# Per-head exponentials with a bias instead of a matmul that subtracts the peak; second norm inside the attention loop, last tokens under the shared network

## The chip, the cores and the metric

One core of one Trainium2 chip runs the whole kernel in one launch. The metric is the time of one execution in microseconds (us) on the device, the median of several runs. Engines are named as the profile names them: PE is TensorE (PEld its weight loads), DVE is VectorE, ACT is ScalarE, POOL is GpSimd, SP issues most of the DMAs.

## The reference

The input `x` has 16 blocks of 128 tokens, each token with 256 features.

```
x = x + tanh(g_xattn) * xattn(layernorm(x), ctx)     # 16 heads of 16 features in each block of 128 tokens
    attn  = gamma * (Q K^T / 4) + delta * (alpha_pos * max(D,0) + alpha_neg * min(D,0))
    D     = clip(frac_k - frac_q, -0.2, 0.2);   probs = softmax(attn);   out = probs V;   out @ Wo.T + bo
x = x + tanh(g_ffn) * ffn(layernorm(x))
    8 experts (256 -> 1024 -> 256, exact gelu), the best 2 of each token by the gate's scores,
    weighted with the softmax over these 2, and a shared network of the same size for every token
```

Every matrix product is made of three bf16 products (high by high, high by low, low by high part), so each operand is split: ACT makes the high part with a copy, DVE or POOL subtracts it to get the low part.

## The kernel before, in words

The program is written out by hand for each engine, with semaphores; each engine works through its own list in order. A wait at the head of a list holds everything behind it. It has these stages.

1. Projections of keys, values and queries.
2. Attention: a loop over 32 half blocks `u`, two for each block `b` of 128 tokens (a token block below). Each `u` has two groups of four heads, so `n = 2u` and `2u+1`, each a tile of 128 queries by 4x128 keys. PE makes scores (`scores`), DVE takes the largest of each head (`peaks`, L830), turns it to two bf16 parts (L833, L835), PE turns these round (`turn_peaks`), ACT copies them (`peaks_moved`, L631), PE subtracts them from the scores with two 512-column matmuls (`subtract_peaks`), ACT takes one exponential of 128x512 (`exponent`, L623), PE turns the result round (`turn_probs`, L1270), ACT copies the high part (`probs_high`, L627), DVE the low part (`probs_low`, L840), PE multiplies with the values (`weigh_values`). Once for each block there follow `output`, `turn_o`, `outputs_high`, `outputs_low`, `project_o`, `residual`. ACT and POOL also convert one piece of the expert weights for each block (`piece_high`, L619; `piece_low`, L487), and prepare the differences of the bias table (`clip`, L472 and L473; `top_part`, L653; `split_difference`, L480).
3. The second norm, its transposition and the gate's scores in eight pairs of blocks (`norm2`, `turn2`, `high2`, `low2`, `gate`), after the attention loop.
4. The shared network: 32 steps `m` (4 groups of 512 tokens by 8 parts of the hidden width). PE runs `shared_up(m+2)` and `shared_down(m)`, six 512-column and twelve 256-column matmuls. ACT makes the gelu (L725) and its high part (L734), POOL (the first 8 steps) or DVE the low part. Beside it DVE chooses the experts, counts the rows of each, and gives every row a place (L990 to L1047); PE's step 8 needs DVE's split, which in DVE's list stands behind this choice. Then DVE builds the rows (`payload`) and POOL sends them out with indirect DMAs (L544). Further weight pieces are loaded (SP, L347: piece `m` waits until piece `m-2` is converted, as there are two buffers) and converted.
5. The experts: 39 tiles of 128 rows (`body`). PE runs up(j), turns tile j+2, and down(j-1).

A weight piece is 128x1024 of fp32, 512 KB; there are 36 of them, four for each network. `store_group` writes the result of the shared network, and `b2f` (1 MB, L425) is loaded by SP when the last of these four writes has landed.

## Time and profile before

| | |
|---|---|
| median of 3 runs | 586.01 us (585.37 to 590.19) |
| the profiled execution, its own time | 587.57 us |
| its span in the trace | 585.7 us |
| mean granted clock of PE | 0.953 of full speed |

The span is what the trace shows of that execution; the 1.9 us beside it lie before and after. Differences are worked out within the span and then applied to the median.

### The profile page before, as it was taken

To read this page: it belongs to the slowest core of one execution; us is meant where nothing else is said; L and a number is where in the kernel's file an instruction comes from. 1 tells how busy PE (TensorE), PEld (TensorE's weight loads), DVE (VectorE), ACT (ScalarE), POOL (GpSimd) and SP (SyncE) were. 2 spreads that over 40 slices of the span, in tenths; PEclk is the share of its full clock that TensorE was granted. 3 is DMA by queue.
4 is the path that set the end of the run, shared out by engine and by line. 5 is a ranking of instruction groups with operands and counts; after the bars stand their busy time and mean duration, and the time that the engine had idled before them with its cause. 6 is when DMAs were issued, how large, how long until landed. Compare 5 with 4: busy or idle time off the path is not lost.

```text
span 585.7 us, 17314 instructions
## 1 busy us (share of the span) xinstructions
PE 516.2 (88%) x6424; PEld 421.7 (72%) x6425; DVE 408.1 (70%) x972; ACT 309.3 (53%) x722; POOL 262.1 (45%) x193
## 2 busy tenths in 40 slices
PE   2698699899999997599679999999999999999990
PEld 0354477777777776456346668899999999999990
DVE  4965648787878788969848748666666666666660
ACT  3656546666666665468336665444544544444430
POOL 4344527575757653459566624322323323323322
PEclk9889969999999999879798999999999999999996
DMA  9500012233323341134253685322223233222121
GB/s 278 199 1 5 1 41 88 65 106 120 96 69 102 118 130 37 41 105 139 87 172 126 197 179 186 66 45 54 38 51 54 36 53 54 36 54 53 28 29 18
DMA packets 37554, 49.17 MB, mean 84 GB/s; under 512 B 8066, under 2 KB 30722, under 8 KB 37380
## 3 DMA queue, kind: packets, MB, share of 16 engines
q1 hardware_dynamic: 30356, 39.18, 22.5%
q0 software_dynamic: 7152, 9.34, 8.7%
q8 instruction: 33, 0.54, 0.4%
q14 instruction: 13, 0.11, 0.1%
HBM read 31.79 MB, written 16.72 MB: 83 GB/s over the span
## 4 chain that ended last, share of the span: by engine, by line
PE 64%; DVE 23%; ACT 4%; DMA 3%; issue 3%; POOL 1%; SPq 0%; POOLq 0%; DVEq 0%; ACTq 0%
PE bank L1172 59%; DVE mx L830 4%; DVE W L840 3%; PE bank L1270 3%; DVE W L805 2%; PE bank L1433 1%; ACT W L627 1%; DVE m L833 1%; DMA xres<-x 1%; DVE xres L861 1%; DVE hbuf L960 1%; DVE st L863 1%; DVE xres L812 1%; DMA xres<-xs_dram 1%; POOL rstd L444 1%
## 5 line engine op out<-in xcount | busy, mean ns | idle before, releaser
L762 ACT ACTIVATE hbuf<-bank,b1t 128x128 f32<-128x128 f32 x312 | 88.7, 368 | 112.2 <-PE bank L1172 109.6
L1172 PE MATMUL bank<-W,xT 128*128 (+1 forms) x1704 | 136.5, 249 | 0.4 <-DVE xT L1128 0.4
L1172 PE MATMUL bank<-xres,W 128*128 128x128 bf16 (+1 forms) x1920 | 124.7, 224 | 9.5 <-DVE xres L812 9.2
L563 POOL DMA_INDIRECT out<-xres,idu x39 | 60.7, 1557 | 156.3 <-DVE xres L1147 147.2
L1172 PEld LDWEIGHTS bank<-xres,W 128*128 (+1 forms) x1920 | 111.9, 98 | 18.6 <-issue 8.8
L1172 PEld LDWEIGHTS bank<-W,xT 128*128 128x128 bf16 (+1 forms) x1704 | 113.9, 97 | 14.4 <-issue 1.0
L1172 PE MATMUL bank<-W 128*128 128x17 bf16 (+3 forms) x1440 | 86.2, 207 | 3.2 <-DVE W L840 1.5
L1172 PEld LDWEIGHTS bank<-W 128*128 128x128 bf16 x1440 | 67.8, 98 | 16.6 <-DVE W L840 2.7
L487 POOL TENSOR_TENSOR W<-stage,W 128x1024 bf16<-128x1024 f32 x28 | 60.6, 2167 | 39.8 <-ACT W L619 31.8
L1172 PE MATMUL bank<-W,hsplit 128*128 128x256 bf16 x432 | 57.3, 283 | 9.3 <-DVE hsplit L1089 5.5
L1172 PEld LDWEIGHTS bank<-W,hsplit 128*128 128x128 bf16 x432 | 43.7, 102 | 24.1 <-DVE hsplit L1089 6.2
L840 DVE TENSOR_TENSOR W<-bank,W 128x512 bf16<-128x512 f32 x64 | 41.3, 686 | 26.2 <-ACT W L627 26.2
L1128 DVE TENSOR_TENSOR xT<-hbuf,xT 128x512 bf16<-128x512 f32 x78 | 54.0, 693 | 2.7
L1172 PE MATMUL bank<-xT,W 128*128 128x512 bf16 x192 | 51.3, 409 | 0.0
L1126 DVE CAST xT<-hbuf 128x512 bf16<-128x512 f32 x78 | 34.4, 441 | 21.1 <-ACT hbuf L762 19.5
L830 DVE TENSOR_REDUCE mx<-bank 128x4 f32<-128x512 f32 x64 | 40.9, 680 | 7.7 <-PE bank L1172 7.7
L544 POOL DMA_INDIRECT xs_dram<-W,place x32 | 36.8, 1150 | 19.1 <-DVE W L1059 10.2
L623 ACT ACTIVATE W<-bank 128x512 f32<-128x512 f32 x64 | 34.7, 594 | 19.2 <-PE bank L1172 19.2
L1270 PE MATMUL bank<-cst,W 128*128 128x128 f32 x256 | 41.1, 285 | 0.3 <-ACT W L623 0.3
L725 ACT ACTIVATE hbuf<-bank,col 128x512 f32<-128x512 f32 x32 | 21.9, 683 | 35.9 <-PE bank L1172 17.0
L619 ACT ACTIVATE W<-stage 128x1024 bf16<-128x1024 f32 x36 | 37.5, 1043 | 3.4 <-DMA stage<-wts 3.4
L480 POOL TENSOR_TENSOR W<-W 128x512 bf16<-128x512 f32 x16 | 18.5, 1156 | 43.2 <-ACT W L653 43.1
(153 smaller groups left out, 662.7 us busy)
## 6 DMA issues: line engine op xcount, KB each, us to landing
stage<-wts SPq DMA_DIRECT2D x36, 512.0 KB
xres<-xs_dram SPq DMA_DIRECT2D x39, 128.0 KB, 2.1
xs_dram<-hbuf SPq DMA_DIRECT2D x7, 645.0 KB, 6.5
W<-ctxT SPq DMA_DIRECT2D x4, 512.0 KB, 6.0
xres<-x SPq DMA_DIRECT2D x4, 512.0 KB, 7.9
out<-xres SPq DMA_DIRECT2D x4, 512.0 KB, 5.3
W<-wproj SPq DMA_DIRECT2D x4, 256.0 KB, 6.8
hsplit<-frac SPq DMA_DIRECT2D x16, 64.0 KB, 5.8
```

Of the source, the lines that this page charges most:

```text
L487: nc.gpsimd.tensor_tensor(lo, stage[:, k * HID:(k + 1) * HID], hi, ALU.subtract).then_inc(converted, 1)
L544: nc.gpsimd.indirect_dma_start(xs_dram, bass.IndirectOffsetOnAxis(place[:, b % 4, k:k + 1], axis=0), pay[:, b % 4, k, :], None).then_inc(d ...
L563: nc.gpsimd.indirect_dma_start(out, bass.IndirectOffsetOnAxis(idu[:, par, t:t + 1], axis=0), ysb[par][t], None, compute_op=ALU.add).then_i ...
L619: nc.scalar.activation(W[:, piece_at(i, k):piece_at(i, k) + HID], stage[:, k * HID:(k + 1) * HID], ACT.Copy).then_inc(conv_hi, 1)
L623: nc.scalar.activation(sc[n % R], psS[n % R][:], ACT.Exp).then_inc(probs, 1)
L762: ins = nc.scalar.activation(hbuf[:, q, c * TR:(c + 1) * TR], bank[UPS * par + q][:, c * TR:(c + 1) * TR], ACT.Gelu, bias=b1t[:, par, UC * ...
L830: nc.vector.tensor_reduce(mx[:, u % 2, HR * i:HR * (i + 1)], psS[n % R][:].rearrange("p (j t) -> p j t", t=T), AX.X, ALU.max).then_inc(pea ...
L840: nc.vector.tensor_tensor(pTl[n % 2], psT[n % 2][:], pTh[n % 2], ALU.subtract).then_inc(pt_lo, 1)
L1126: nc.vector.tensor_copy(hi, hbuf[:, q, :]).then_inc(h_hi, 1)
L1128: nc.vector.tensor_tensor(lo, hbuf[:, q, :], hi, ALU.subtract).then_inc(h_ready, 1)
L1172: return nc.tensor.matmul(o, a, b, start=start, stop=stop, **kw)
L1270: ins = nc.tensor.transpose(psT[n % 2][:, j * T:(j + 1) * T], sc[n % R][:, j * T:(j + 1) * T], ident)
```

## The change

- The weights of the queries are scaled with -gamma/4 and the slopes with -1, so that PE makes negated scores. DVE takes the smallest of each head. ACT takes the exponential of one head each (128x128) with scale -1 and this minimum as its bias, four instructions in the place of one. `turn_peaks`, `peaks_moved`, `subtract_peaks` and their tables go.
- The second norm runs inside the attention loop, one block at a time, two to three blocks behind: statistics on DVE (`stats2`, `aggregate2`), four small POOL instructions (`deviation2`), the norm itself on ACT (`norm2`, was DVE), `turn2`, `inputs2_high` and `inputs2_low`.
- After the loop PE starts the shared network at once. The gate's scores of the first 12 blocks, and the last block's output, norm and scores stand between its first steps (`last_tokens`).
- DVE chooses in two parts. The counting is made by PE (31 matmuls of 8 to 120 columns beside the one that was there, after step 5), and DVE's chain for it is shorter. DVE splits the hidden tiles from step 5 on (POOL did to step 7), and these splits stand between the parts of the choice.
- The conversions of weights move: pieces 16 to 19 stand at steps 3, 4, 6 and 8 on ACT and are finished on POOL (18 and 19 between the sending of rows); 20 to 31 stand at steps 10 to 28 on ACT, finished on DVE; 32 to 35 are converted inside the first four tiles of the experts on ACT and POOL, and are loaded after `b2f`.
- The loop over tiles is cut in two, so that PE waits for the last piece only at tile 16.

```diff
-POOL_PIECES_AT = (1, 3, 4, 6, 7)
-VECTOR_PIECES = range(PIECES - 12, PIECES - 4)
-HIGHS_AT = (10, 11, 13, 15, 18, 20, 22, 23)
-LOWS_AT = (11, 12, 14, 16, 19, 21, 23, 24)
-LAST_HIGHS_AT = (28, 30)
+POOL_PIECES_AT = (2, 3)
+DISPATCH_PIECES_AT = (1, 3)
+PIECES_AT = (3, 4, 6, 8)
+VECTOR_PIECES = range(NOW + 4, PIECES - 4)
+HIGHS_AT = (10, 11, 13, 14, 16, 17, 19, 20, 22, 24, 26, 28)
+LOWS_AT = (11, 12, 14, 15, 17, 18, 20, 21, 23, 25, 27, 29)
-POOL_SPLITS = HC
+POOL_SPLITS = 5
+RANKS_AT = 5
...
(sync)
             store_group(3)
             sp.wait_ge(out_written[3], 16)
             sp.dma_start(b2f, b2.to_broadcast([P, E * D])).then_inc(ld_b2, 16)
-            with sp.Fori(2, TILES // 2) as i:
+            load_pieces(PIECES - 4, PIECES - 2)
+            load_tile(4, 0)
+            load_piece(PIECES // 2 - 1, 0)
+            load_tile(5, 1)
+            load_piece(PIECES // 2 - 1, 1)
+            with sp.Fori(3, TILES // 2) as i:
...
(gpsimd)
+            def deviation2(b):
+                pool.wait_ge(ln2_stat, b + 1)
+                link(inverse_deviation(rstd2, mv2, b, b + 1))
+                link(nc.gpsimd.tensor_tensor(nmr2[:, b:b + 1], mv2[:, b:b + 1, 0], rstd2[:, b:b + 1], ALU.mult))
+                nc.gpsimd.tensor_scalar(nmr2[:, b:b + 1], nmr2[:, b:b + 1], -1.0, None, ALU.mult).then_inc(ln2_rstd, 1)
...
             for m in range(POOL_SPLITS):
+                if m == 2:
+                    deviation2(B - 1)
...
+                if b in DISPATCH_PIECES_AT:
+                    q = NOW + 2 + DISPATCH_PIECES_AT.index(b)
+                    piece_low(q // 2, q % 2)
...
-            add_tile(0, 0)
-            add_tile(1, 1)
+            for j in range(4):
+                piece_low((PIECES - 4 + j) // 2, j % 2)
+                add_tile(j, j % 2)
...
(scalar)
             def exponent(n):
-                act.wait_ge(sub_ps, n + 1)
-                nc.scalar.activation(sc[n % R], psS[n % R][:], ACT.Exp).then_inc(probs, 1)
+                act.wait_ge(peak, n + 1)
+                for j in range(HR):
+                    at = HR * (n % 2) + j
+                    ins = nc.scalar.activation(sc[n % R][:, j * T:(j + 1) * T], psS[n % R][:, j * T:(j + 1) * T], ACT.Exp,
+                                               scale=-1.0, bias=mx[:, n // 2 % 2, at:at + 1])
+                ins.then_inc(probs, 1)
...
+            def norm2(b):
+                act.wait_ge(ln2_rstd, b + 1)
+                if b:
+                    act.wait_ge(x2T_ps, b)
+                nc.scalar.activation(xh2, xres[:, b * D:(b + 1) * D], ACT.Identity,
+                                     scale=rstd2[:, b:b + 1], bias=nmr2[:, b:b + 1]).then_inc(xh2_ready, 1)
...
+                if m in PIECES_AT:
+                    q = NOW + PIECES_AT.index(m)
                     piece_high(q // 2, q % 2)
...
                 gelu_tile(j, par)
                 if more == 2:
                     high_tile(j + 2, par)
+                if isinstance(j, int) and j < 4:
+                    piece_high((PIECES - 4 + j) // 2, j % 2)
...
(vector)
+            choose(0, EARLY_TOKENS)
+            inputs2_low(B - 1)
+            link(choose(EARLY_TOKENS, B))
+            split_shared(5)
...
(tensor)
             piece_converted(pe, 3)
             shared_up(0)
             shared_up(1)
+            turn_o(B - 1)
+            turn2(B - 3)
+            gate(0, EARLY_TOKENS)
             for m in range(HC * GROUPS):
                 if m + 2 < HC * GROUPS:
                     shared_up(m + 2)
...
                 shared_down(m)
+                last_tokens(m)
```

## Rows read from the trace of the kernel before

**Rows 1.** Windows by stage: span, busy time and count of each engine, granted clock, DMA.

```profile
78.27:229.70 151.43, 141.06 (x2414) 116.50 (x2414) 119.53 (x258) 99.01 (x200) 88.60 (x55) 0.98 0.31 94
229.70:252.92 23.22, 13.60 (x211) 11.88 (x209) 21.03 (x54) 9.68 (x17) 10.52 (x8) 0.81 0.21 69
252.92:353.32 100.40, 91.11 (x577) 58.04 (x574) 72.67 (x199) 59.52 (x84) 62.47 (x48) 0.91 0.48 141
367.86:555.76 187.90, 187.90 (x2518) 177.75 (x2518) 123.11 (x309) 86.07 (x304) 53.61 (x35) 1.00 0.27 47
```

**Rows 2.** Timeline of PE in one token block of the attention loop.

```profile
158.79 0.66 PE L1270 MATMUL bank<-cst,W 128*128 128x128 f32 x4
...
161.05 1.20 PE L1172 MATMUL bank<-W 128*128 128x512 bf16 x26
...
163.57 0.22 PE L1172 MATMUL bank<-idb,m 128*16 128x128 bf16 x1 [0.61 <-DVE m L835]
```

**Rows 3.** Timeline of ACT in the same token block.

```profile
154.28 1.05 ACT L627 ACTIVATE W<-bank 128x512 bf16<-128x512 f32 x2
155.24 0.71 ACT L653 ACTIVATE W<-W,cst 128x512 bf16<-128x512 f32 x1
...
161.48 1.09 ACT L623 ACTIVATE W<-bank 128x512 f32<-128x512 f32 x2 [0.41 <-PE bank L1172]
```

**Rows 4.** Groups by line and form, ACT: busy us, mean ns of one, idle before.

```profile
L762 ACT ACTIVATE hbuf<-bank,b1t 128x128 f32<-128x128 f32 x312 | 88.7, 368 | 112.2 <-PE bank L1172 109.6 <-DVE xT L1128 2.3
...
L619 ACT ACTIVATE W<-stage 128x1024 bf16<-128x1024 f32 x36 | 37.5, 1043 | 3.4 <-DMA stage<-wts 3.4
...
L645 ACT ACTIVATE W<-xres,nmr,rstd 128x256 f32<-128x256 f32 x16 | 8.3, 589 | 16.9 <-POOL nmr L463 16.9
...
L637 ACT ACTIVATE W<-bank 128x256 bf16<-128x256 f32 x16 | 5.8, 360 | 1.2 <-PE bank L1292 1.2
```

**Rows 5.** Groups by line and form, POOL's powers.

```profile
L444 POOL TENSOR_TENSOR rstd<-rstd,mhalf 128x4 f32<-128x4 f32 x5 | 5.7, 1149 | 0.4
...
L444 POOL TENSOR_TENSOR rstd<-rstd,mhalf 128x12 f32<-128x12 f32 x1 | 2.3, 2297 | 0.1
```

**Rows 6.** Timelines of DVE and PE at the start of attention.

```profile
71.36 1.29 DVE L830 TENSOR_REDUCE mx<-bank 128x4 f32<-128x512 f32 x2 [2.00 <-PE bank L1172]
...
73.56 0.27 PE L1172 MATMUL bank<-idb,m 128*16 128x128 bf16 x1 [2.30 <-DVE m L835]
...
78.27 1.11 PE L1270 MATMUL bank<-cst,W 128*128 128x128 f32 x4 [0.26 <-ACT W L623]
...
99.41 0.60 PE L1270 MATMUL bank<-cst,W 128*128 128x128 f32 x4
```

**Rows 7.** Group by line and form: PE's down matmuls of the shared network.

```profile
L1172 PE MATMUL bank<-W,hsplit 128*128 128x256 bf16 x432 | 57.3, 283 | 9.3 <-DVE hsplit L1089 5.5 <-issue 3.5 <-POOL hsplit L533 0.3
```

**Rows 8.** Timeline of PE in the shared network, its up matmuls.

```profile
307.67 2.77 PE L1172 MATMUL bank<-xT,W 128*128 128x512 bf16 x6
...
328.13 1.46 PE L1172 MATMUL bank<-xT,W 128*128 128x512 bf16 x6
...
330.73 1.46 PE L1172 MATMUL bank<-xT,W 128*128 128x512 bf16 x6
```

**Rows 9.** Timelines of POOL and ACT: a conversion, a send, a load's wait.

```profile
269.42 2.13 POOL L487 TENSOR_TENSOR W<-stage,W 128x1024 bf16<-128x1024 f32 x1
...
284.03 1.35 POOL L544 DMA_INDIRECT xs_dram<-W,place  x1 [4.96 <-DVE W L1059]
...
274.76 1.06 ACT L619 ACTIVATE W<-stage 128x1024 bf16<-128x1024 f32 x1 [0.92 <-DMA stage<-wts]
```

**Rows 10.** Timelines of SP and PE at the experts' start; the issue of `b2f`.

```profile
362.20 0.33 SPq L425 DMA_DIRECT2D xres<-b  x1
...
363.99 2.85 PE L1172 MATMUL bank<-xres,W 128*128 128x128 bf16 x48
...
xres<-b SPq DMA_DIRECT2D x1, 1024.0 KB, 4.8
```

More of the change, by code:

```diff
@@ L59 @@
 C_I32 = C_TILE + TILES
-C_IND = C_I32 + KB
-C_POS, C_NEG, C_TOP, C_LOW, C_FLOOR, C_CEIL, C_SECOND = (C_IND + 2 * HR + k for k in range(7))
+C_POS, C_NEG, C_TOP, C_LOW, C_FLOOR, C_CEIL, C_SECOND = (C_I32 + KB + k for k in range(7))
 C_N = C_SECOND + 1
@@ L124, in build @@
         cab = [under(H * KB, bf16) for _ in range(2)]
-        ind = under(2 * HR * T, bf16)
-        mts = [under(T, bf16) for _ in range(2)]
         brows = under(4 * D, bf16)
@@ L282, in wait_alone, with tiles @@
             eng.sem_inc(passed[name], 1)
-        def tiles(eng, body):
-            body(0, 0, 2)
-            body(1, 1, 2)
-            with eng.Fori(1, TILES // 2 - 1) as i:
+        def tiles(eng, body, late=None):
+            for j in range(4):
+                body(j, j % 2, 2)
+            with eng.Fori(2, LATE_TILES // 2) as i:
+                body(2 * i, 0, 2)
+                body(2 * i + 1, 1, 2)
+            if late:
+                late()
+            with eng.Fori(LATE_TILES // 2, TILES // 2 - 1) as i:
                 body(2 * i, 0, 2)
@@ L565, in add_tile @@
                         ysb[par][t], None, compute_op=ALU.add).then_inc(added[t], 16)
-            add_tile(0, 0)
-            add_tile(1, 1)
-            with pool.Fori(1, TILES // 2) as i:
+            for j in range(4):
+                piece_low((PIECES - 4 + j) // 2, j % 2)
+                add_tile(j, j % 2)
+            with pool.Fori(2, TILES // 2) as i:
                 add_tile(2 * i, 0)
@@ L985, in _ @@
-            low2(PAIRS - 2, (PAIRS - 2) % 3)
-            low2(PAIRS - 1, (PAIRS - 1) % 3)
-            dve.wait_ge(gate_ps, B)
-            link(nc.vector.tensor_tensor(lg, bank[5][:, 0:B * E].rearrange("p (b e) -> p b e", e=E),
-                                         row[:, V_GB:V_GB + E].rearrange("p (o e) -> p o e", o=1).to_broadcast([P, B, E]), ALU.add))
-            for b in range(B):
-                ins = nc.vector.max(mx8[:, b, :], lg[:, b, :])
-            link(ins)
-            for b in range(B):
-                ins = nc.vector.max_index(ix8[:, b, :], mx8[:, b, :], lg[:, b, :])
@@ L997, in _, with split_shared @@
-            link(ins)
+            output(B - 1)
+            residual(B - 2)
+            stats2(B - 2)
+            aggregate2(B - 2)
+            outputs_low(B - 1)
+            inputs2_low(B - 3)
+            residual(B - 1)
+            stats2(B - 1)
+            aggregate2(B - 1)
+            inputs2_low(B - 2)
+            def split_shared(m):
+                dve.wait_ge(sh_hi, m + 1)
+                nc.vector.tensor_tensor(hsplit[:, m % DEEP, 1, :], hbuf[:, m % DEEP, :], hsplit[:, m % DEEP, 0, :],
+                                        ALU.subtract).then_inc(sh_ready[1], 1)
@@ new lines, in choose @@
+            def choose(lo, hi):
+                dve.wait_ge(gate_ps, hi)
+                link(nc.vector.tensor_tensor(lg[:, lo:hi], gate_bank(lo)[:, lo * E:hi * E].rearrange("p (b e) -> p b e", e=E),
+                                             row[:, V_GB:V_GB + E].rearrange("p (o e) -> p o e", o=1).to_broadcast([P, hi - lo, E]),
+                                             ALU.add))
+                for b in range(lo, hi):
+                    ins = nc.vector.max(mx8[:, b, :], lg[:, b, :])
+                link(ins)
+                for b in range(lo, hi):
+                    ins = nc.vector.max_index(ix8[:, b, :], mx8[:, b, :], lg[:, b, :])
+                return ins
@@ L1232, in scores @@
                     pe.wait_ge(d_ready, b + 1)
-                for i in (1, 0):
-                    if i == 0 and u:
-                        pe.wait_ge(mT_ready, u)
+                for i in range(2):
                     if u >= 2:
@@ L1303, in project_o, with turn2 @@
                 mm(psM[:, D:2 * D], oneb[:], brows[:, 3 * D:4 * D], False, True).then_inc(y_ps, 1)
+            def turn2(b):
+                pe.wait_ge(xh2_ready, b + 1)
+                if b >= B - 3:
+                    pe.wait_ge(x2_lo, b)
+                y = x2_ps(b)
+                for c in range(DC):
+                    ins = nc.tensor.transpose(y[:, c, :], xh2[:, c * P:(c + 1) * P], ident)
+                ins.then_inc(x2T_ps, 1)
             pe.wait_ge(ld_cst, 16)
```

355 lines of the change are left out of this document (152 added, 203 removed).

## The prediction

> **What bounds the kernel now.** I read the windows by stage first, then the timelines of each engine inside one stage, then the groups by line for durations. The windows [rows 1] show what matters where. In attention PE is busy 141.06 of 151.43 us. In the stage between (second norm and gate, 23.22 us) it is busy 13.60 us while DVE has 21.03: this is a bubble of PE. In the shared network it is busy 91.11 of 100.40, at a clock of 0.91. In the experts it is busy all the time, in a steady cadence with a clock of 1.00; the change doesn't touch what a tile costs there, so this stage moves as a whole.
>
> The attention loop takes (99.41 - 78.27) = 21.14 us for its first two token blocks [rows 6] and from there to the last pair's transposes at 229.70 [rows 1] it is 13.5 blocks, 9.65 to 9.72 each. In its timeline PE's instructions stand close together; the only gap is one of 0.61 for each block where it waits for the peaks on DVE [rows 2]. ACT has gaps before the exponentials [rows 3]. So PE and the chain of the peaks set the period of 9.72.
>
> **Part 1, exponentials by head.** PE loses, for each token block, four 512-column matmuls and two turned peaks. Of the 26 matmuls that start at 161.05, 24 are the small ones, so I take 0.21 for each of the two big ones: 4 x 0.21 = 0.85; two turned peaks with 0.15 each, and the 0.61 of waiting [rows 2]. It gains the two transposes of the second norm, 0.26. 9.72 - 0.85 - 0.3 - 0.61 + 0.26 = 8.2 us is what PE would need.
>
> ACT takes the bound over. Its nearest row to a 128x128 exponential with a bias is the experts' gelu: 368 ns for one, and 88.7/312 = 284 ns of busy time, so fours of 1.14 [rows 4]. A step from one to the next is (1.137 - 0.368)/3 = 0.256, so an exponent takes 4 x 0.256 = 1.03 of ACT, where the 512-wide one takes half of 1.09 less its overlap, 0.49 [rows 3]. For one block: four exponents 4.10; four copies of probabilities 4 x 0.48 = 1.92 (two in 1.05 with their tail) [rows 3]; the weight piece 0.94, the top part 0.61, the output 0.27, the new norm 0.50 and the new transposed copy 0.28, each its mean less 0.1 of overlap [rows 3, 4]. Sum 8.62. Of waits two remain: the second copy of a pair needs PE's transposes of the second exponent, 0.66 long [rows 2], while the first copy covers only 0.48 and the semaphores take 0.1 to 0.2, so some 0.37 twice. That is 9.36 for one block, ACT in one go. DVE loses the small peak instructions and gains two small ones; POOL gains `deviation2`, by interpolation from 1.15 for 4 columns and 2.30 for 12 [rows 5] 0.72 for the power and by estimate another 1.0 for the three small ones and their links: 1.7. POOL is busy for 88.60 of 151.43 us [rows 1], 5.7 for a block; with 1.7 it is 7.4. Both stay under 9.36. Behind POOL's wait for the statistics stands the split of the differences; it moves by 1 us and still comes 1 us before PE needs it, so I cost that at nothing.
>
> The page "ScalarE: Activation LUTs" of the Trainium skill (section on what ACT_TABLE_LOAD costs) says that an activation with a pointer for its bias takes about 280 ns + 0.833 ns for each element, with 93 ns of overlap: an estimate of 0.294 for a step. By this, which speaks against the change, the period would be about 10.0 and the loop slower than now. The rows have 0.256 for the same shape and operands, so the trace is better than the page here, and its number decides.
>
> So 13.5 blocks give 0.36 each, -4.9. The start of the loop gives more. Now the first peaks wait 2.30, the clock falls for ten us after it, and the first transposes start at 78.27 [rows 6]. After the change: first reduce 71.36 to 72.05, four exponentials 1.14, transposes at 73.25, -5.0. PE has the second scores in between and no long wait, so that I expect no fall of the clock there, and the first two blocks take 17.3 for 21.1 (ACT's cadence with less in it), -3.8. Together -13.7, by which the last pair's transposes start at 216.
>
> **Part 2, the stage between.** It goes. From the last pair's transposes to the first shared matmul there remain: the second exponent and its transposes 1.5, copy 0.57, low part 0.69, weighing 0.31, output projection 0.75, links: 4.5 for 23.2 [rows 1], -18.7. What is late next is the shared network's own feeding.
>
> **Part 3, shared network.** A step of PE is 2.60 (328.13 to 330.73) [rows 8]; from first up to last down 82. Now it takes 100.4 [rows 1]: 5.5 of waiting for DVE's choice and 3.5 of "issue" [rows 7], and some 8 at half clock behind these gaps and at its start (2.77 for 1.46) [rows 8]. The waiting for the choice goes (a split stands between its parts). Added to PE: twelve gates, four late ones, three norms' and one output's transposes, the projection and the counting, 16 x 0.27 + 1.0 + 0.75 + 1.2 = 7.3. The last block's chain (projection, residual, POOL, norm, transposes, gate) runs beside steps 0 to 3, each link ready when PE comes to it; I cost its waits at 0.5. If that cover failed, each us would count.
>
> New waits come from the weight pieces. ACT's list has piece 20 at step 10. Its load waits for piece 18 to be converted, and POOL does this only after sending the rows of block 1. I lay out the choice: scores of the last gate some 19 us after the shared network starts; max, index, one-hots to 24; counting on PE, then seven small DVE instructions, places, weights, first payload at 33.5. Four sends of 1.3 to 1.65 each, conversion 2.13, load 3.2 (from the end of a conversion at 271.55 to 274.76) [rows 9]: the piece lands at 45, while ACT is there at 34.5. ACT stands 10 us, and behind it the gelu of step 11; PE has two steps in hand and loses 3.1 at step 10 (DVE's table and accumulation before its split) and 4.5 at step 11. Piece 21 waits likewise for piece 19 behind blocks 2 and 3: 4.7 at step 12. After it, twelve pieces in two buffers with a turn-around of 3.2 + 1 + 1.2 are just above PE's cadence: 1.7 more. Sum 14.0, and 2.5 for the clock behind it. 82 + 7.3 + 0.5 + 14.0 + 2.5 = 106.3 against 100.4, +5.9. For the load I know 2.8 to 4.2, which makes 1.6 less or 3 more.
>
> **Part 4, start of the experts.** Before, the last pieces were through when tile 0 began. Now ACT has piece 32 behind the gelu of tile 0, and SP issues its load after `b2f`, which waits for the last write: 362.2 at its earliest, 4.8 to land, and the piece queued behind it some 1.7 more, so 368.7, less 1 since the write comes a little earlier. Conversion 0.94, half the gelu 1.14, its split 1.2: PE can go on with down(1) at 371, where it was at 363.99 [rows 10]. Some 0.6 of that is there already, as PE waited for tile 4. +6.5, and +2 for the clock behind a wait of 7 us. Pieces 33 to 35 come in time by the same layout. The bound from below is nothing (if the load were early), from above 11. The cut loop costs nothing, since PE is busy for the whole of the stage, over the exit of the loop that is there [rows 1].
>
> Sum: -13.7 - 18.7 + 5.9 + 8.5 = -18.0. Span 585.7 to 567.7, this execution, with the 1.9 beside its span, 587.57 to 569.6, the median of the runs, 1.6 lower, 586.01 to 568.0.
>
> **The rivals.**
> A. The loads are not late: the choice is quick enough, or the DMA queues empty enough, that parts 3 and 4 lose no more than half of 14 + 2.5 + 8.5. For it speaks that I stack many small durations; against it that piece 32 can't be loaded before the last write. 586 - 30 = 556, down to 550.
> B. PE's "issue" gap comes back. In the trace PE stood for 3.5 [rows 7] and ran at half clock behind it, 2.77 for 1.46 and a like loss after [rows 8], in the middle of the sending of rows. I left it out, since in the new order the sends are held up by payloads; with it, or with one more fall of the clock, 568 + 8 = 576, up to 582.
> C. The exponentials don't overlap as the gelus do, and ACT's step is the full 0.368. Then each block takes 16 x 0.112 = 1.8 more, 16 blocks 28.7: 597, slower. Its place is ACT in attention; it decides from 0.07 more for each instruction on, a step of 0.33. Against it stands the row of 312 gelus with the same source, target and bias [rows 4].
> D. PE's clock falls in the loop, as it is now busy 8.2 of 9.36. Rows of gaps of 0.61 have a clock of 0.98 to 1.00 [rows 1, 2], the falls followed gaps of 2.3 and more [rows 6 to 8]. A part of the loop at half clock costs 10 or more: about no change.
>
> **How the numbers follow.** Forecast 0.47 (561 to 574), A 0.2, B 0.2, C 0.05, D 0.05, the rest unnamed. A change of 1% (5.9 us) is about what a measurement of this kernel can tell from none. Faster by that: forecast, A, nearly all of B, 0.86; within it 0.08; slower 0.06. The range leaves out C, D and the far end of A: 551 to 582.
>
> **What would show it.** Right: a period of 9.4 in attention with ACT in one go and the gaps on PE waiting for ACT; the first shared matmul near 220; ACT idle for about 10 us before its 21st weight copy, "DMA stage"; a wait of PE of 6 to 8 us at down(1); the experts' tiles unchanged. Wrong: exponents in fours over 1.3, PE waiting for POOL's splits in steps 3 and 4, or a first payload much before 250.

## The result, and the profile after

The changed kernel takes 571.38 us (571.14 to 571.98, 4 runs) where the kernel before took 585.69 on the same chip (582.32 to 590.19, 4 runs): a ratio of 0.975, interval 0.970 to 0.979, so 2.5% faster. The forecast was 568.0 in a range of 551 to 582. A later repeat, beside e5 to e7, gave 571.36 us (570.98 to 573.16) and a ratio of 0.974 (0.966 to 0.982). The profiled execution took 571.98 us, its span is 570.1 us, the mean granted clock 0.964.

The windows of the changed kernel by stage, the first three cut at the same instructions as [rows 1]: attention from the first to the last pair's transposes, the stage between, the shared network up to its last down matmuls; then the experts' start up to down(5) (the down matmuls of the sixth tile), and the steady tiles. Columns as in [rows 1].

```profile
74.21:217.87 143.66, 126.41 (x2346) 109.46 (x2346) 109.71 (x224) 134.83 (x380) 106.65 (x109) 1.00 0.34 99
217.87:223.66 5.79, 4.58 (x40) 3.18 (x41) 2.74 (x7) 3.33 (x9) 1.86 (x5) 0.51 0.26 91
223.66:329.11 105.45, 93.56 (x744) 61.65 (x743) 68.69 (x201) 62.93 (x91) 57.05 (x49) 0.96 0.43 129
329.11:374.41 45.30, 37.94 (x484) 33.74 (x482) 31.88 (x53) 20.38 (x63) 14.99 (x8) 0.92 0.39 114
374.41:541.00 166.59, 166.59 (x2230) 157.59 (x2228) 110.94 (x276) 77.54 (x275) 47.96 (x31) 1.00 0.27 47
```

In attention ACT, the fourth engine column, is now the busiest with 134.83 of 143.66 us; it had 99.01 of 151.43. The bubble between is 5.79 us and was 23.22. The shared network is 5.05 us longer, and PE isn't always busy in the first 45 us of the experts, where it stands or runs slower for some 9 us. Nothing changed in the steady tiles: from down(5) to the end of the span it is 195.7 us, and was 195.8.

ACT in one token block of attention:

```profile
149.46 1.06 ACT L637 ACTIVATE W<-stage 128x1024 bf16<-128x1024 f32 x1
150.41 0.60 ACT L673 ACTIVATE W<-xres,nmr,rstd 128x256 f32<-128x256 f32 x1
150.90 2.17 ACT L643 ACTIVATE W<-bank,mx 128x128 f32<-128x128 f32 x8
152.89 0.66 ACT L649 ACTIVATE W<-bank 128x512 bf16<-128x512 f32 x1
...
157.97 1.08 ACT L649 ACTIVATE W<-bank 128x512 bf16<-128x512 f32 x2 [0.34 <-PE bank L1270]
158.94 1.06 ACT L637 ACTIVATE W<-stage 128x1024 bf16<-128x1024 f32 x1
```

The weight copy comes at 149.46 and 158.94: a period of 9.48 us, where it was 9.65 to 9.72. Eight exponentials take 2.17 us, one takes 0.398 (the group below), so that one step is (2.17 - 0.398)/7 = 0.253 us. These groups by line and form stand beside [rows 4] and [rows 7]:

```profile
L788 ACT ACTIVATE hbuf<-bank,b1t 128x128 f32<-128x128 f32 x312 | 88.6, 368 | 110.3 <-PE bank L1184 102.3 <-DVE xT L1140 7.6
L643 ACT ACTIVATE W<-bank,mx 128x128 f32<-128x128 f32 x256 | 69.6, 398 | 2.2 <-DVE mx L856 2.2
L637 ACT ACTIVATE W<-stage 128x1024 bf16<-128x1024 f32 x36 | 38.0, 1055 | 38.0 <-DMA stage<-wts 34.9 <-issue 3.1
...
L1184 PE MATMUL bank<-W,hsplit 128*128 128x256 bf16 x432 | 54.4, 276 | 11.9 <-DVE hsplit L1000 11.5 <-POOL hsplit L552 0.4
```

ACT's waits for weight loads went from 3.4 us [rows 4] to 34.9. PE, where it needs a split of the shared network, stood 9.3 us before, of which 3.5 were "issue" [rows 7], and stands 11.9 now. ACT and PE in the shared network show the chain, first ACT:

```profile
267.59 1.06 ACT L637 ACTIVATE W<-stage 128x1024 bf16<-128x1024 f32 x1 [10.54 <-DMA stage<-wts]
...
274.95 1.06 ACT L637 ACTIVATE W<-stage 128x1024 bf16<-128x1024 f32 x1 [5.07 <-DMA stage<-wts]
```

and PE:

```profile
264.62 1.68 PE L1184 MATMUL bank<-W,hsplit 128*128 128x256 bf16 x12 [3.75 <-DVE hsplit L1000]
...
271.99 2.19 PE L1184 MATMUL bank<-W,hsplit 128*128 128x256 bf16 x12 [3.13 <-DVE hsplit L1000]
...
278.03 1.48 PE L1184 MATMUL bank<-W,hsplit 128*128 128x256 bf16 x12 [1.58 <-DVE hsplit L1000]
```

These waits have a second cause beside the late loads. The two splits that PE waits for at 264.62 and 271.99 are these rows of DVE:

```profile
261.96 2.60 DVE L1000 TENSOR_TENSOR hsplit<-hbuf,hsplit 128x512 bf16<-128x512 f32 x1
...
269.91 2.02 DVE L1000 TENSOR_TENSOR hsplit<-hbuf,hsplit 128x512 bf16<-128x512 f32 x1 [4.52 <-ACT hsplit L761]
```

and over them lie POOL's conversions of pieces 18 and 19:

```profile
261.65 2.36 POOL L517 TENSOR_TENSOR W<-stage,W 128x1024 bf16<-128x1024 f32 x1
...
269.24 2.13 POOL L517 TENSOR_TENSOR W<-stage,W 128x1024 bf16<-128x1024 f32 x1
```

Elsewhere such a split takes 0.69 us. So 1.9 of PE's 3.75 us and 1.3 of its 3.13 come from DVE being held up while POOL converts; the repeat of the kernel shows the same (2.61 and 1.84).

PE at the experts' start:

```profile
344.65 0.69 PE L1444 MATMUL bank<-cst,xres 128*128 128x128 f32 x2 [2.59 <-DMA xres<-xs_dram]
347.54 4.51 PE L1184 MATMUL bank<-W,xT 128*128 x24 [2.20 <-DVE xT L1140]
...
368.48 2.79 PE L1184 MATMUL bank<-W,xT 128*128 x24 [1.61 <-DVE xT L1140]
```

DVE there:

```profile
351.21 3.31 DVE L1138 CAST xT<-hbuf 128x512 bf16<-128x512 f32 x1
...
358.03 3.31 DVE L1138 CAST xT<-hbuf 128x512 bf16<-128x512 f32 x1
...
364.64 3.77 DVE L1140 TENSOR_TENSOR xT<-hbuf,xT 128x512 bf16<-128x512 f32 x1
```

and POOL:

```profile
351.50 2.72 POOL L517 TENSOR_TENSOR W<-stage,W 128x1024 bf16<-128x1024 f32 x1
...
358.38 2.67 POOL L517 TENSOR_TENSOR W<-stage,W 128x1024 bf16<-128x1024 f32 x1
...
365.17 2.68 POOL L517 TENSOR_TENSOR W<-stage,W 128x1024 bf16<-128x1024 f32 x1
```

Here is the piece that the forecast had right in its sum and wrong in its parts. Down(1), at 347.54, is late by ACT's wait for the 33rd piece, as forecast. But behind it three DVE instructions of 0.43 or 0.69 us take 3.3 to 3.8, each of them over a conversion on POOL; PE waits again at 368.48. A fourth stands ahead of down(1): DVE's cast at 345.15 takes 1.52 us, over the conversion at 344.27.

### The profile page after: what moved, and what is told of

Same layout as the page of the kernel before. It is cut to its first block, busy times and chain, and to the rows that moved or that the text cites. A ratio compares the mean times of both kernels' runs of the same rounds, so it can differ in the third digit from the quotient of the medians.

```text
span 570.1 us, 17300 instructions
## 1 busy us (share of the span) xinstructions
PE 493.2 (87%) x6358; PEld 408.4 (72%) x6359; DVE 381.7 (67%) x890; ACT 344.2 (60%) x906; POOL 266.9 (47%) x243
## 4 chain that ended last, share of the span: by engine, by line
DMA 24%; PE 20%; ACT 20%; DVE 17%; issue 11%; POOL 4%; DVEq 1%; POOLq 1%; SPq 0%; ACTq 0%
DMA out<-xres,idu 19%; PE bank L1184 16%; ACT W L643 7%; DMA stage<-wts 4%; PE bank L1270 4%; ACT W L637 3%; ACT W L649 3%; DVE xres L1159 2%; ACT W L684 2%; DVE xT L1138 2%; DVE W L831 2%; POOL W L517 2%; POOL xs_dram L563 2%; DMA xres<-x 1%; ACT W L673 1%
## 5 line engine op out<-in xcount | busy, mean ns | idle before, releaser
L1184 PEld LDWEIGHTS bank<-xres,W 128*128 (+1 forms) x1920 | 112.0, 98 | 21.4 <-issue 11.9
L1184 PE MATMUL bank<-W 128*128 128x17 bf16 (+2 forms) x1376 | 72.0, 197 | 8.4 <-DVE xT L899 4.9
L517 POOL TENSOR_TENSOR W<-stage,W 128x1024 bf16<-128x1024 f32 x24 | 53.0, 2209 | 40.3 <-ACT W L637 38.2
L1184 PEld LDWEIGHTS bank<-W 128*128 128x128 bf16 x1376 | 61.1, 97 | 15.1 <-DVE W L878 5.4
L643 ACT ACTIVATE W<-bank,mx 128x128 f32<-128x128 f32 x256 | 69.6, 398 | 2.2 <-DVE mx L856 2.2
L1184 PE MATMUL bank<-W,hsplit 128*128 128x256 bf16 x432 | 54.4, 276 | 11.9 <-DVE hsplit L1000 11.5
L1138 DVE CAST xT<-hbuf 128x512 bf16<-128x512 f32 x78 | 43.0, 552 | 27.7 <-ACT hbuf L788 26.7
L637 ACT ACTIVATE W<-stage 128x1024 bf16<-128x1024 f32 x36 | 38.0, 1055 | 38.0 <-DMA stage<-wts 34.9
L1184 PEld LDWEIGHTS bank<-W,hsplit 128*128 128x128 bf16 x432 | 41.8, 98 | 26.5 <-DVE hsplit L1000 16.2
L1140 DVE TENSOR_TENSOR xT<-hbuf,xT 128x512 bf16<-128x512 f32 x78 | 57.1, 732 | 2.7
L563 POOL DMA_INDIRECT xs_dram<-W,place x32 | 40.3, 1258 | 24.4 <-DVE W L1072 16.5
L649 ACT ACTIVATE W<-bank 128x512 bf16<-128x512 f32 x64 | 37.9, 612 | 9.4 <-PE bank L1270 9.0
L1270 PEld LDWEIGHTS bank<-cst,W 128*128 128x128 f32 x256 | 28.3, 143 | 20.7 <-ACT W L643 20.4
```

The source lines that it names most:

```text
L517: nc.gpsimd.tensor_tensor(lo, stage[:, k * HID:(k + 1) * HID], hi, ALU.subtract).then_inc(converted, 1)
L563: nc.gpsimd.indirect_dma_start(xs_dram, bass.IndirectOffsetOnAxis(place[:, b % 4, k:k + 1], axis=0), pay[:, b % 4, k, :], None).then_inc(d ...
L637: nc.scalar.activation(W[:, piece_at(i, k):piece_at(i, k) + HID], stage[:, k * HID:(k + 1) * HID], ACT.Copy).then_inc(conv_hi, 1)
L643: ins = nc.scalar.activation(sc[n % R][:, j * T:(j + 1) * T], psS[n % R][:, j * T:(j + 1) * T], ACT.Exp, scale=-1.0, bias=mx[:, n // 2 % 2 ...
L649: nc.scalar.activation(pTh[n % 2], psT[n % 2][:], ACT.Copy).then_inc(pt_hi, 1)
L1138: nc.vector.tensor_copy(hi, hbuf[:, q, :]).then_inc(h_hi, 1)
```

## The experiments

The experiments ran on three chips. The kernel before took 580.41 us on the chip of e1 to e4, 587.07 on that of c, e5, e6 and e7, and 580.26 on that of e8 to e11. The changed kernel took 571.4 in the first comparison (585.69 for the kernel before) and in c; on the chips of e1 to e4 and of e8 to e11 it didn't run. Differences to it are therefore read from the windows by stage. In the stages that an edit doesn't touch they agree: e1 has the last pair's transposes at 217.37, where the changed kernel has them at 217.87, and needs 241.5 us from the last down matmuls to the end of its span, where the changed kernel needs 241.0. The same kernel differs by about 1 us in the shared network (105.45 in the first trace, 106.34 in c's).

**c: the changed kernel again**, beside e5, e6 and e7.

> The changed kernel once more, beside the next three and on their chip, as what they are measured against. From the first comparison (ratio 0.975 to the kernel before) it should take 565 to 567 us where the kernel before takes 580.4; the two cheap repairs timed so far (567.3 and 564.8) would then have gained nothing in time although their profiled spans are 5 us shorter than that of the changed kernel on the first chip (564.9 and 565.4 against 570.1). If instead it takes 569 to 571, the repairs gained what their spans say and the ratio varies by chip.

Measured: 571.36 us, span 571.2. The number is that of the second case, but the run can't decide between the two, since the kernel before takes 587 us on this chip and not 580: the ratio, 0.974, is that of the first comparison. That the repairs gained what their spans say rests on the windows.

**e1: the conversions out of the sends.** Pieces 18 and 19, whose conversion by POOL stood between the sends, are converted ahead of them.

```
+            for q in (NOW + 2, NOW + 3):
+                piece_low(q // 2, q % 2)
             pool.wait_ge(pad_written, PADS)
...
-                if b in DISPATCH_PIECES_AT:
-                    q = NOW + 2 + DISPATCH_PIECES_AT.index(b)
-                    piece_low(q // 2, q % 2)
```

> The changed kernel with weight pieces 18 and 19 finished on POOL before it sends the first rows, where they stood between the sends of blocks 1 and 3. Theory (the loads of pieces 20 and 21 are late because their buffers are freed behind the sends): ACT's waits of 10.54 and 5.07 us for them shrink to under 2, PE's waits of 3.75, 3.13 and 1.58 at steps 10 to 12 shrink to some 3 for DVE's accumulation before split 10, the half clock behind them goes, and the kernel is 7 to 9 us faster than 571.4: 562 to 564. Rival (DVE's tile table and accumulation before split 10 are what holds PE, and the load is hidden behind them): under 3 us, 569 or more. Second rival (the stall only moves, since the 12 pieces after it are bound by the turn-around of two buffers): the gain at step 10 is given back by step 28, 569 or more, with ACT's waits for loads spread over the steps.

Measured: 567.27 us (564.62 to 568.71), span 564.9. ACT's waits of 10.54 and 5.07 us became 2.25 and 1.30, so the loads were late for the reason that I had given. The shared network takes 100.2 us (its first up matmul has no record and starts at some 223.2; the last down matmuls at 323.38), 5.2 less than 105.45, not the 8 or so that 562 to 564 us asked for. The rest stayed at another place. DVE's timeline in e1:

```profile
248.81 1.43 DVE L1034 TENSOR_SCALAR te_i<-te_i 128x8 int32<-128x8 int32 x1
...
252.12 2.45 DVE L1045 TENSOR_TENSOR W<-W 128x128 f32<-128x128 f32 x2
```

Its PE:

```profile
265.37 2.74 PE L1183 MATMUL bank<-W,hsplit 128*128 128x256 bf16 x12 [3.19 <-DVE hsplit L999]
```

And its POOL:

```profile
248.07 2.13 POOL L517 TENSOR_TENSOR W<-stage,W 128x1024 bf16<-128x1024 f32 x1 [4.59 <-ACT W L636]
252.29 2.13 POOL L517 TENSOR_TENSOR W<-stage,W 128x1024 bf16<-128x1024 f32 x1 [2.09 <-ACT W L636]
```

In the changed kernel the same two instructions of the choice take 0.17 and 0.49. POOL's conversion, put ahead of the sends, held them for 3.2 us together, and the choice is what everything behind waits for. The splits of steps 10 and 11 are no longer held (0.71 and 0.68 us for 2.60 and 2.02). So POOL's hold on DVE moved, from two splits to two instructions of the choice, and the 5.2 us are not the loads' part alone.

**e2: the loads before the tiles.** Pieces 32 and 33 are loaded right after the third group's write, ahead of the loads of tiles 2 and 3 and of `b2f`.

```
             store_group(2)
+            load_pieces(PIECES - 4, PIECES - 2)
             load_tile(2, 0)
...
-            load_pieces(PIECES - 4, PIECES - 2)
```

> The changed kernel with the loads of pieces 32 and 33 issued before tile 2 is loaded, ahead of the last write and b2f. Theory (ACT's wait of 8.32 us for piece 32 holds the gelu of tile 1, and PE with it): this wait goes, PE's waits of 2.59 and 2.20 us in tile 2 and the half clock behind them (4.51 for 2.78) go, while the waits of DVE for POOL's conversions in tiles 2 to 4 (0.3, 1.6 us on PE) stay: 5 to 7 us faster, 564.5 to 566.5. Rival (the write of group 3 and b2f are held up by the same traffic, so that the wait moves to tile 4's rows or to the bias): under 2 us.

Measured: 564.82 us (563.12 to 567.23), span 565.4. That is within the theory's 564.5 to 566.5. Down(1) starts 13.8 us behind the last down matmuls (330.40 to 344.20), not 18.4, and at full clock. The edit does two things here: piece 32 comes early, and so do the rows of tile 4, whose load stood behind the pieces (PE's wait for them, 2.59 us, became 0.50). With the rows as late as before, down(1) could have started at some 16.2 us at the earliest, so 2.4 of the 4.6 us needed them too. PE's waits of 0.41 and 1.61 us behind DVE's long instructions stayed, so they are a second cause.

**e3: one exponential for four heads.** It leaves out that each head has its own minimum: the first head's serves all four.

```
-                for j in range(HR):
-                    at = HR * (n % 2) + j
-                    ins = ...Exp of 128 columns, bias=mx[:, n // 2 % 2, at:at + 1])
+                at = HR * (n % 2)
+                ins = nc.scalar.activation(sc[n % R], psS[n % R][:], ACT.Exp, scale=-1.0, bias=mx[:, n // 2 % 2, at:at + 1])
```

> The changed kernel with one exponential of 128x512 for four heads, all with the first head's minimum as bias, so that three of four heads are shifted by another head's peak: this part of the computation is changed. Theory (ACT is what sets the period of 9.48 us of a token block, and its four exponents cost 4.1 us of it): ACT loses about 4 x (1.03 - 0.58) = 1.8 for each block, PE with 8.2 to 8.5 sets the period; 16 blocks give 14 to 18 us: 554 to 557. Rival (PE or DVE is as near to the bound as ACT): less than 8 us, period over 9.0. The skill's page on ScalarE would say the exponents cost 0.294 a step and so the same direction with 0.6 more.

**e4: five exponentials for four heads.** The first head's is made in two halves of 64 columns.

```
-                for j in range(HR):
+                for lo, hi in ((0, 64), (64, 128), (128, 256), (256, 384), (384, 512)):
```

> The changed kernel with the first head of each exponent in two halves of 64 columns, five instructions for four, same result. Theory (ACT bounds the loop, each instruction costs 0.15 us of fixed time besides 0.8 ns for a column): 64 exponents x 0.15 = 9.8 us more, 580 to 582, the period 10.1. Rival (ACT has slack behind the chain through PE and DVE): under 3 us more.

Measured: e3 553.65 us (552.94 to 554.36), e4 580.54 us (579.67 to 583.88). The weight copy of ACT shows the period in e3, and one of e4:

```profile
147.72 1.06 ACT L637 ACTIVATE W<-stage 128x1024 bf16<-128x1024 f32 x1
...
155.33 1.09 ACT L647 ACTIVATE W<-bank 128x512 bf16<-128x512 f32 x2 [1.25 <-PE bank L1268]
156.30 1.06 ACT L637 ACTIVATE W<-stage 128x1024 bf16<-128x1024 f32 x1
```

```profile
155.54 1.06 ACT L637 ACTIVATE W<-stage 128x1024 bf16<-128x1024 f32 x1
...
165.58 1.05 ACT L637 ACTIVATE W<-stage 128x1024 bf16<-128x1024 f32 x1
```

With 0.45 us less by estimate for each exponent of four heads on ACT the period is 8.58, and ACT now waits 1.25 us for PE. PE in turn stands for 0.42 us in a block, behind DVE's split of the turned inputs (L897), so that ACT isn't the bound there; e11 below reaches 8.37. With four small instructions more in a block (0.15 us each: ten take 2.48 us, eight took 2.17) it is 10.04. The time follows ACT's sum in both directions: in the changed kernel ACT is the bound of attention. 16 x 0.56 = 9.0 us are the period, and e4's median is 9.2 above the changed kernel's. The profiled execution was the slowest of e4's, 12.0 us more of span; the clock in it was 0.95 from 145 to 218 us where it was 1.00. The ratio to the kernel before is 1.000 on this chip: one more ACT instruction for each four heads is what this change can bear there before it gains nothing.

**e5: part 1 alone.** The kernel before, with only the exponentials by head and what they need (negated scores, minima for maxima); no norm in the loop, the old order of the rest.

```
             def exponent(n):
-                act.wait_ge(sub_ps, n + 1)
-                nc.scalar.activation(sc[n % R], psS[n % R][:], ACT.Exp).then_inc(probs, 1)
+                act.wait_ge(peak, n + 1)
+                for j in range(HR):
+                    at = HR * (n % 2) + j
+                    ins = nc.scalar.activation(sc[n % R][:, j * T:(j + 1) * T], psS[n % R][:, j * T:(j + 1) * T], ACT.Exp,
+                                               scale=-1.0, bias=mx[:, n // 2 % 2, at:at + 1])
+                ins.then_inc(probs, 1)
...
(peaks_moved, turn_peaks and subtract_peaks go, with DVE's two small instructions for each unit)
```

> The kernel before with only the first part of the change: scores negated, one exponential for each head with its minimum as bias, the turned peaks and their matmuls, moves and splits gone; second norm, shared network and loads as before. Theory (the sum of the engines' work per token block sets the period): ACT has in a block what it has in the changed kernel (9.48) less the norm's activation (0.50) and the move of the turned inputs (0.26), 8.7; DVE and PE have less than that, so the block falls from 9.72 to 8.6-8.8, 16 blocks give 15 to 18 us, the start of attention 4 to 5 more: 558 to 562 us where the kernel before takes 580.4, ratio 0.962 to 0.968. That is more than the whole change gains. Rival 1 (the exponentials' gain is the start alone, and the period hangs on waits between engines that stay): 9.5 or more for a block, 572 to 576. Rival 2 (the stages behind it lose it again by loads that are not there yet): the attention as in the theory, but the total 565 to 570.

Measured: 562.29 us (559.22 to 565.98), span 564.2, ratio 0.957. ACT's weight copy comes at 153.38 and 162.03, a period of 8.65, as in the theory. So part 1 alone gives more than the whole change, by 9 us in the medians and 5.9 in the spans. The windows say where: the first shared matmul is at 231.12 against 223.66, so the parts behind part 1 give 7.5 there; but they cost 3.9 in the shared network (101.6 against 105.5) and 9.6 up to down(5) (35.7 against 45.3). In the shared network PE again stands for 3.7 us in gaps marked "issue" among its down matmuls, as in the kernel before (3.5).

**e6: the last lows on DVE.** e2, and DVE converts the low parts of the last four pieces behind its tiles 0, 1 and 3.

```
+TILE_PIECES = ((PIECES - 4,), (PIECES - 3,), (), (PIECES - 2, PIECES - 1))
...
             for j in range(4):
-                piece_low((PIECES - 4 + j) // 2, j % 2)
                 add_tile(j, j % 2)
...
(DVE, behind low_tile)
+                    for q in TILE_PIECES[j]:
+                        piece_low(q)
```

> Changed kernel with the order of loads of e2_load_before_tiles, and the low parts of the last four weight pieces computed on DVE (1.2 us each) behind its tiles 0, 1 and 3 where GpSimd computed them in 2.7 us each. Theory (while GpSimd works on 128x1024 in SBUF, a DVE cast from SBUF to bf16 stands still: 3.3 us for 0.42): the casts of 2.25, 3.31, 3.32 and 3.78 us in the tiles become 0.42 to 0.69, and PE's waits behind them (0.41, 1.61 and the issue gaps of 0.20 and 0.26) go: 2.5 us less than e2, a span near 563. Rival (the long casts have another cause, and DVE's 4 x 1.22 us come on top): casts stay over 2 us, time as e2 or 1 to 3 us longer.

Measured: 561.19 us (560.30 to 562.66), span 559.3. DVE in e6 in this stage:

```profile
336.56 0.42 DVE L1141 CAST xT<-hbuf 128x512 bf16<-128x512 f32 x1
...
343.26 0.66 DVE L1141 CAST xT<-hbuf 128x512 bf16<-128x512 f32 x1
...
349.69 2.35 DVE L905 TENSOR_TENSOR W<-stage,W 128x1024 bf16<-128x1024 f32 x2
```

and its PE:

```profile
341.61 2.78 PE L1190 MATMUL bank<-W,xT 128*128 x24
...
347.14 2.78 PE L1190 MATMUL bank<-W,xT 128*128 x24
...
363.71 2.78 PE L1190 MATMUL bank<-W,xT 128*128 x24
```

The long casts are gone though DVE does 4.8 us more, and PE is in its steady cadence from the second tile on: down(5) comes 35.1 us behind the last down matmuls, 10.2 less than in the changed kernel. That is 3.9 less than in e2, more than the 2.5 expected: all of PE's small gaps went too, with them a wait of 0.50 us for the rows of tile 4.

**e7: the norm on DVE.** The norm of token blocks 0 to 12 is computed by DVE, behind `output`, where DVE waited 0.36 us.

```
(ACT)
-                    if b >= 3:
-                        norm2(b - 3)
(DVE)
+                nc.vector.tensor_scalar(xh2, xres[:, b * D:(b + 1) * D], mv2[:, b:b + 1, 0], rstd2[:, b:b + 1],
+                                        ALU.subtract, ALU.mult).then_inc(xh2_ready, 1)
```

> Changed kernel, but the second norm inside the attention (tokens 0 to 12) is computed by DVE (0.37 us, as in its payload rows) in a place where it waits 0.36 us per block, not by ACT (0.50 us per block). Theory (ACT's sum of 9.48 us is the period): 8.98 to 9.05 us a block, 13 blocks, 5.5 to 6.5 us less than the changed kernel. Rival 1 (period set by waits between PE, DVE and ACT, of which ACT's 0.34 and 0.26 for PE are the sign): the freed 0.50 becomes a longer wait for PE, period 9.3 to 9.5, gain 0 to 2 us. Rival 2 (DVE's added 0.37 sits on the path): 9.5 to 9.85, up to 5 us slower.

Measured: 563.60 us (562.64 to 565.65), span 560.8.

```profile
155.28 1.06 ACT L637 ACTIVATE W<-stage 128x1024 bf16<-128x1024 f32 x1
156.22 2.17 ACT L643 ACTIVATE W<-bank,mx 128x128 f32<-128x128 f32 x8
...
163.30 1.08 ACT L649 ACTIVATE W<-bank 128x512 bf16<-128x512 f32 x2 [0.34 <-PE bank L1278]
164.27 1.06 ACT L637 ACTIVATE W<-stage 128x1024 bf16<-128x1024 f32 x1
```

The period is 8.99: the 0.50 us that left ACT left the period whole, and the 0.34 that ACT waits for PE didn't grow. Beside c on the same chip the kernel gains 7.8 us, more than the 5.5 to 6.5 expected. 13 x 0.49 = 6.4 are the period; another 1.1 is the stage between, which takes 4.64 us (210.80 to 215.44) at a granted clock of 1.00, where it is 5.79 at 0.51 in the changed kernel.

**e10: two lows on DVE.** Pieces 18 and 19 as in e1, but on DVE, piece 18 before the counting, piece 19 behind the first four payloads.

```
             split_shared(6)
+            piece_low(NOW + 2)
...
+            piece_low(NOW + 3)
             tile_table()
```

> Changed kernel, but the low parts of pieces 18 and 19, which GpSimd computes between its sends, are computed by DVE (1.2 us each): piece 18 ahead of the counting of the choice, piece 19 behind the first four payloads. In e1_low_before_send GpSimd computed them ahead of the sends, and DVE instructions of the choice stood still meanwhile (1.43 us for 0.17, 2.45 for 0.49, 3.2 in all), after which PE waited 0.98, 0.54 and 3.19 us. Theory (the late loads and the held choice were the two costs of this place): the shared network takes 98 to 101 us (105.5 in the changed kernel, 101.1 in e1), 564 to 567 us. Rival (what PE waits for is the row of DVE work itself, payloads and the accumulation behind them, and 2.4 us of conversions make it longer): 102 to 104 us, 568 to 570.

Measured: 563.71 us (562.02 to 565.93), span 563.3. The shared network takes 100.3 us (222.91 to 323.17), within what the theory asked; but e1's is 100.2, not the 101.1 of the expectation, and so nothing is gained over e1 in the stage as a whole. PE still waits 3.64 us for the split at 265.15: DVE works from 249.25 to 264.41 almost without a gap, at its conversions of pieces 18 and 19 (1.23 and 1.21 us), the counting, four payloads, the table of tiles and the accumulation, ahead of that split. For this wait the rival was right: the split itself takes 0.69 us for 2.60, but DVE's own two conversions ahead of it take 2.4. What both e1 and e10 gain are the waits of 3.13 and 1.58 us at steps 11 and 12. Of these 1.3 us were the held split; the loads have the rest, and the half clock behind. No run separates the two causes.

**e9, e8: the repairs together.** e9 is e6, e7 and e1 in one kernel, e8 is e6, e7 and e10; their edits are those above.

> e6 (loads before tiles, last four lows on DVE), e7 (norm on DVE) and e1 (pieces 18 and 19 converted by GpSimd before the sends) together. Theory (three separate stages, so their gains add: 10.2, 7.8 and 4.2 us off 571.4): 549 us, 547 to 551. Rival (an earlier attention brings the shared network on before its weights are loaded: e7's stage then loses up to half its gain): 552 to 556.

> As e9, with pieces 18 and 19 on DVE as in e10. Theory: e9 less what e10 gains over e1 (0 to 3 us), 546 to 549 us. Rival: loads of pieces 20 to 25 bound the stage, which DVE or GpSimd converting two pieces doesn't change: as e9 within 1 us.

Measured: e9 549.59 us (548.45 to 550.74), e8 547.91 us (547.32 to 549.28). The gains add up as the theory had them. e8's shared network is 1.8 us shorter than e9's (99.2 for 101.0), which is most of its lead, and which e10 against e1 didn't show. Part of this is the stage's start, where PE runs at the lower clock for a different time in each run: up to the third group of up matmuls e8 takes 7.1 us and e9 5.9, e10 7.4 and e1 5.9. Behind that point e8 is 3.0 us shorter than e9, and e10 1.4 shorter than e1. The 1.6 us between these two differences stay open. The windows of e8:

```profile
73.88:209.49 135.61, 123.12 (x2319) 108.29 (x2319) 112.85 (x235) 126.77 (x362) 106.17 (x108) 1.00 0.35 105
215.86:315.05 99.19, 92.36 (x746) 61.97 (x744) 68.08 (x203) 63.35 (x91) 53.22 (x47) 0.97 0.50 148
315.05:350.57 35.52, 35.18 (x485) 33.10 (x482) 27.74 (x61) 20.45 (x63) 6.84 (x5) 1.00 0.44 118
```

**e11: one exponential with a common minimum.** e8, with one reduction over four heads and one exponential of 512 columns.

```
-                    nc.vector.tensor_reduce(mx[:, u % 2, HR * i:HR * (i + 1)], ...(j t) -> p j t..., AX.X, ALU.min)
+                    nc.vector.tensor_reduce(mx[:, u % 2, HR * i:HR * i + 1], psS[n % R][:], AX.X, ALU.min)
```

> As e8, with one exponential 512 wide for four heads whose bias is the minimum over all four (one reduction to 128x1 in place of one to 128x4); the softmax divides by the sum, so that the shift cancels unless the peaks of four heads lie so far apart that one underflows. Theory (in e3_wide_exp the period was 8.58 with PE as the bound; e7 had 8.99): 16 blocks by 0.41 us and less at the start and end: 6 to 8 us under e8, 538 to 542 us. Rival (PE waits for peaks or DVE, now that DVE has the norm too): period 8.8 or more, 3 us or less under e8.

Measured: 535.00 us (533.28 to 537.05), span 532.2, ratio 0.922 (0.919 to 0.925): 6.4% under the changed kernel's 571.4, measured on other chips (5.4% by the two ratios to the kernel before). It is 12.9 us under e8, 5 more than expected. The period is 8.37 (ACT's weight copies at 147.62 and 155.98), not 8.58, and the first shared matmul comes at 203.51 against 215.86 in e8; with 16 x 0.62 = 9.9 for the period, another 2.4 lie at the start and the end of attention, the shared network takes 2 less, and the tiles' start 0.4 more. The shift by a common minimum cancels in the division, as long as no head's peak lies so far below another's that its exponentials vanish; for such data it isn't the same computation.

## Why the prediction was right, and where not

Attention: the mechanism held, ACT became the bound (e3, e4 and e7 each moved the period with ACT's sum). The forecast period was 9.36, it is 9.48. The exponentials' step, estimated from the gelu rows as 0.256, is 0.253. ACT's work is 8.88 for 8.62, most of it in the copies of the probabilities (2.13 a block where I had 1.92), and its waits for PE 0.60 for 0.74. The start of the loop came at 74.21, and no fall of the clock after it. The last pair's transposes came at 217.87, forecast 216: -11.8 us, not -13.7. Of the 1.9 us missing, 0.9 were lost ahead of the loop, as the first reduction starts at 72.29 and not at 71.36; the first two blocks took 17.39 for 17.3. The other 0.8 lie in the base: the next 13.5 blocks fell from 130.29 to 126.27 us, 4.0 for 4.9, since before they took 9.65 each and not the 9.72 that the sum used, and after 9.35 on average.

What the text didn't see is what it had bundled. Its 8.2 us for PE and 8.62 for ACT held the norm as a small item; e7 shows that on the engine that bounds each of its 0.5 us counts whole, once for each of the 13 blocks whose norm runs in the loop. The rule of the Trainium skill, page "ScalarE: Activation LUTs", that I weighed (0.294 for a step, period 10.0) fails here by rows of the changed kernel itself, 0.253 for 256 exponentials.

The stage between: 5.8 us are left where I had 4.5, since the clock is at its lower level there (0.51 in the window): -17.4 for -18.7. I had costed durations at the upper level, though PE has pauses of 0.98 and 0.52 us just before. At the upper level the 4.5 was right: e7, where the clock didn't fall, takes 4.64.

The shared network: 105.45 for 106.3. ACT's waits of 10.54 and 5.07 us stand where the layout put them ("ACT stands 10 us"). PE's waits are 11.9 us for 14.5, and the half clock, here and at the start of the stage, cost some 3.8 (PE's rows at 223.66, 264.62, 266.09, 271.99 and 273.97 against their lengths at full clock) for 2.5. But the terms inside don't agree: 3.75, 3.13, 1.58 and then 3.0 us of waits, for 3.1, 4.5, 4.7 and 1.7. And 3.2 us of the first two are the splits that POOL's conversions held, a cause that stands nowhere in my sum. So the waits that are left to the late loads at steps 11 and later are some 6.4 us where I had 10.9, and the hold made up for a part of it. e1 and e10 show that taking POOL's conversions out of the sends gains 5.2 us here, by both causes together; the wait of 3.75 at the split of step 10, which I had named "DVE's table and accumulation", stays without the late loads, at 3.19 and 3.64. The "issue" gap of rival B came back in e5 (3.7 us), which keeps the old order of this stage, and in no run with the new order. So it goes with the old order of the stage; what makes it stays open.

The experts' start: the sum was right, 8.8 us for 8.5 (45.30 to down(5), before 36.55), and the step had two errors that cancelled. First, the row at 363.99 [rows 10] isn't down(1) but the up matmuls of tile 2. Down(1) was this row of the kernel before:

```profile
367.76 2.79 PE L1172 MATMUL bank<-W,xT 128*128 x24
```

It came 14.44 us behind the last down matmuls; now it comes 18.43 behind. The forecast place of down(1) was nearly right (371 is 17.7 behind the last down matmuls at 353.32), only the row that it was held against was wrong. The delay therefore is 4.0 and not 6.5, 1.1 of it the held cast at 345.15, and its clock 1.7, for 2. PE's waits just before down(1) are 2.59 us (for the rows of tile 4) and 2.20, 4.8 together, where I had named 6 to 8 as a sign. Second, "pieces 33 to 35 come in time" was nearly true of their loads (ACT waits 1.11 us once) but not of their conversions: POOL's work there holds DVE's casts, 3.0 us that stood nowhere in my sum. e2 took away the delay of down(1), e6 the held casts.

So the forecast of the whole is near (span 570.1 for 567.7) in part by luck: in two stages a wait that was priced too high stood in for POOL's hold on DVE, which wasn't priced at all. And I never priced part 1 by itself. With e5 the bill reads -21.5 for part 1 (span 564.2 for 585.7) and +5.9 for all the rest, and each item of the rest can be repaired: e8 takes 547.9 us with all parts in place, 14.4 less than part 1 alone.

## What to carry to other kernels

When a change moves work onto several engines, price each part alone and ask which engine bounds the loop after it: on that engine half a microsecond counts in full for every round, and on another it was free (e7). A conversion or copy on POOL isn't free for DVE even where no semaphore ties them: look for DVE rows that are several times longer than their group's mean before you call a POOL edit hidden. Loads with a chain of buffers belong in the queue ahead of anything that waits for late results (e2). Before a term of a forecast is taken as confirmed, look whether its own wait has the forecast length: the sum of a stage can come out right from wrong terms.

## What the runs showed of the hardware

DVE stood still while POOL worked on a 128x1024 subtraction in SBUF: casts from SBUF to bf16 took 3.31 us for 0.43, subtractions with two SBUF inputs 3.77 and 2.60 for 0.69, a 128x8 integer instruction 1.43 for 0.17 (in e1). With POOL's work moved away (e6) those of the experts' start were back at 0.42 to 0.69. POOL's own instruction took 2.7 us instead of 2.13 there. Not all of DVE's work was held: in attention the batch norm's statistics over 256 columns of SBUF took 0.42 us (at 151.91) in the middle of a POOL conversion (150.91 to 153.04), and two reductions from PSUM at 150.72, partly over it, took their usual 1.28. The Trainium skill, page "SBUF — State Buffer" (section on its two separate sides), says that the two engines share one pair of ports, held exclusively for a whole instruction. The runs agree: the held cast at 351.21 ends at 354.52, POOL's conversion at 354.22.

PE's clock fell to its lower level, 1.2 GHz, behind pauses of 2 to 4 us (4.51 us for 2.78 at 347.54), and also without a long one, behind pauses of 0.98 and 0.52 us around 217 (eight transposes took 2.15 us for 1.04), in the repeat too. In e7 it stayed at 1.00 in the same stage, with waits of 0.98 and 0.38 us at its start. In e8, with no long pause there, the experts' start ran at 1.00.

The kernel before took 580.3 to 587.1 us, by chip; the changed one took 571.4 both times, where the kernel before took 585.7 and 587.1. If it takes 571.4 on the other chips too, as the windows of e1 suggest, the change gains 1.5% there and not 2.5%: an estimate, which wasn't measured. Where in the kernel before the extra time lies isn't known, as it was profiled only in the first comparison.
